# Attention on one core: another order of the score and search pieces within a head

## The reference, cut to what matters

```python
qkv = x @ W_w.T + W_b                                   # x: 2 x 2048 x 256, 16 heads of 16
attn = jnp.einsum('bhqd,bhkd->bhqk', q, k) / jnp.sqrt(jnp.float32(d))
attn = jnp.where(causal[None, None], -jnp.inf, attn)
attn = attn + rpb[rel_idx].transpose(2, 0, 1)[None]     # bias by distance
w = jax.nn.softmax(attn, axis=-1)
o = jnp.einsum('bhqk,bhkd->bhqd', w, v)
```

## Time and profile before

| | |
|---|---|
| median of 3 runs | 2679.14 us (2678.54 to 2680.85) |
| the profiled execution | 2680.85 us, its span 2679.1 us |
| TensorE (PE) busy | 2482.3 us, 93% of the span |
| VectorE (DVE) busy | 1965.3 us, 73% |
| ScalarE (ACT) busy | 1382.1 us, 52% |
| GpSimd (POOL) busy | 1103.8 us, 41% |
| one head of the attention | about 60.5 us |

### The profile page before, as it was taken

How to read it: one execution, slowest core, us unless ns; L and a number is a source line. 1 busy time by engine, 2 the same in 40 slices (tenths; PEclk the granted TensorE clock), 3 DMA queues, 4 the chain that set the end, 5 groups by cost and what they waited for, 6 DMA issues and landing times. The chain is left out here.

```text
span 2679.1 us, 43868 instructions
## 1 busy us (share of the span) xinstructions
PE 2482.3 (93%) x15059; PEld 1557.9 (58%) x15059; DVE 1965.3 (73%) x4039; ACT 1382.1 (52%) x2469; POOL 1103.8 (41%) x1090
## 2 busy tenths in 40 slices
PE   8999999999999999899999996999999999977973
PEld 4433333333333333577777775888888888855762
DVE  3777777777777773456666647999999999973346
ACT  2466666666666666444454536555555555543220
POOL 3522222222222211100001003999999989944543
PEclk9999999999999999999999997999999999987986
DMA  8544323333333411100000000000000000024775
GB/s 244 168 70 75 76 57 57 58 58 58 57 72 70 81 35 66 53 16 17 24 24 16 9 17 8 12 12 12 12 12 12 12 12 12 4 97 146 250 225 170
DMA packets 109601, 166.41 MB, mean 62 GB/s; under 512 B 15876, under 2 KB 74296, under 8 KB 106232
## 3 DMA queue, kind: packets, MB, share of 16 engines
q1 hardware_dynamic: 99064, 143.24, 21.3%
q0 software_dynamic: 6144, 16.79, 2.0%
q10 hardware_dynamic: 4224, 4.19, 0.5%
HBM read 97.66 MB, written 62.01 MB: 60 GB/s over the span
## 5 line engine op out<-in xcount | busy, mean ns | idle before, releaser
L644 ACT ACTIVATE ssm_in_dt<-att_s 128x512 f32<-128x512 f32 (+3 forms) x1280 | 610.0, 535 | 348.1 <-PE att_s L541 183.4
L733 DVE TENSOR_REDUCE att_partmax<-att_s 128x1 f32<-128x512 f32 x768 | 494.1, 685 | 112.7 <-PE att_s L515 66.3
L541 PE MATMUL att_s<-att_qs,att_ks 49*128 49x512 f32 (+3 forms) x1280 | 435.4, 420 | 16.2 <-ACT ssm_in_dt L644 13.8
L515 PE MATMUL att_s<-att_ks,att_qs 49*128 49x512 f32 (+3 forms) x1280 | 435.8, 425 | 4.1 <-DVE att_qs L723 4.1
L1787 POOL TENSOR_TENSOR ssm_cc<-ssm_cc,ssm_h 128x512 f32<-128x512 f32 x256 | 331.8, 1296 | 244.4 <-DVE ssm_h L1844 243.2
L541 PEld LDWEIGHTS att_s<-att_qs,att_ks 49*128 49x128 f32 x1280 | 207.8, 185 | 380.4 <-ACT ssm_in_dt L644 307.5
L432 POOL TENSOR_SCALAR_AFFINE_SELECT ssm_in_dt<-ssm_in_dt 128x256 f32<-128x256 f32 x256 | 104.0, 406 | 619.9 <-ACT ssm_in_dt L644 543.8
L584 PE MATMUL att_o_ps<-ssm_in_dt,att_vst 128*32 128x512 f32 (+3 forms) x2560 | 340.7, 542 | 5.3 <-ACT ssm_in_dt L644 5.3
L1802 POOL TENSOR_TENSOR ssm_out_z<-ssm_out_z,ssm_cc 128x512 f32<-128x512 f32 x256 | 336.8, 1316 | 0.1
L1727 ACT ACTIVATE ssm_cc<-ssm_c_ps,ssm_cur 128x512 f32<-128x512 f32 x256 | 199.3, 778 | 224.7 <-PE ssm_c_ps L1676 224.7
L736 DVE CUSTOM_DVE_ANT_0 att_hid<-att_s,att_hidden 128x512 bf16<-128x512 f32 (+3 forms) x512 | 238.7, 486 | 94.7 <-PE att_s L515 93.9
(11 more groups left out here) (323 smaller groups left out, 4189.6 us busy)
## 6 DMA issues: line engine op xcount, KB each, us to landing
qk_halves<-ssm_in_dt SPq DMA_DIRECT2D x64, 256.0 KB
moe_sorted<-att_hidden SPq DMA_DIRECT2D x31, 512.0 KB, 9.8
moe_rows<-moe_sorted SPq DMA_DIRECT2D x62, 256.0 KB
moe_answers<-moe_mixed SPq DMA_DIRECT2D x62, 256.0 KB
att_far<-bias_tables SPq DMA_DIRECT2D x96, 136.0 KB, 8.2
att_stage_q<-qk_halves SPq DMA_DIRECT2D x96, 128.0 KB, 4.4
att_stage_k<-qk_halves SPq DMA_DIRECT2D x96, 128.0 KB, 6.0
ssm_raw<-in_w_bc SPq DMA_DIRECT2D x30, 256.0 KB, 2.6
```

What stands on the lines that cost most here:

```text
L515: mm = nc.tensor.matmul(s1[:, S1_BANK[at], 0:hi - lo], qs[p % 3][half(b, ROWS), I * P:(I + 1) * P], ks[p % 3][half(b, ROWS), lo:hi], start ...
L541: mm = nc.tensor.matmul(s2[:, turn % RING, 0:hi - lo], ks[p % 3][half(b, ROWS), J * P:(J + 1) * P], qs[p % 3][half(b, ROWS), lo:hi], start ...
L644: nc.scalar.activation(prob[:, b, step % 2, x * CH + lo:(x + 1) * CH], s2[:, turn % RING, 0:CH - lo], ACT.Exp, scale=1.0 / HD).then_inc(s2 ...
L733: nc.vector.tensor_reduce(most, piece, AX, ALU.max).then_inc(s1_read, 1)
```

## The change

It gives other orders to `SCORED` and `SEARCHED`. `SCORED` is now made by a function; the result differs from before in steps 0 and 1 only, where the pieces come in the order of keys. `SEARCHED` keeps its last twelve pieces; of the first 28 most change places. The near groups go with their pieces: they then stand in 0.0, 0.1, 0.3, 1.1, 1.3, 2.1, 3.3, 4.3, 5.0, 5.3, 6.2 and 6.3. The far groups stay where they are. In every slot, the score and the search still have the same number of columns.

```diff
--- before.py
+++ after.py
@@ -125,21 +125,23 @@
 RING = 3
 
 GROUPS_OF_KEYS = ((8, 9), (10, 11), (0,), (1,), (2,), (3,), (4, 12), (5, 13), (6, 14), (7, 15))
-
-
-SCORED = [[(8, 2), (9, 2), (8, 3), (9, 3)], [(11, 2), (10, 2), (10, 3), (11, 3)],
-          [(0, 2), (0, 0), (0, 3), (0, 1)], [(1, 2), (1, 0), (1, 3), (1, 1)],
-          [(2, 2), (2, 0), (2, 3), (2, 1)], [(3, 2), (3, 0), (3, 3), (3, 1)],
-          [(4, 3), (4, 1), (12, 3), (4, 2)], [(5, 3), (5, 1), (13, 3), (5, 2)],
-          [(6, 3), (6, 1), (14, 3), (6, 2)], [(7, 3), (7, 1), (15, 3), (7, 2)]]
-assert [sorted(pieces) for pieces in SCORED] == [[(J, c) for J in keys for c in range(J // TPC, S // CH)] for keys in GROUPS_OF_KEYS]
-SEARCHED = [(15, 0), (14, 3), (15, 1), (15, 2),
-            (12, 3), (13, 3), (13, 0), (12, 2),
-            (8, 0), (15, 3), (14, 0), (14, 2),
-            (12, 1), (10, 2), (12, 0), (13, 2),
-            (9, 0), (9, 2), (11, 1), (11, 2),
-            (13, 1), (8, 2), (10, 0), (9, 1),
-            (11, 0), (8, 1), (14, 1), (10, 1),
+FAR_FIRST = (2, 0, 3, 1)
+
+
+def scored(keys):
+
+    pieces = [(J, c) for J in keys for c in range(J // TPC, S // CH)]
+    return [pieces[n] for n in (FAR_FIRST if keys[0] < FAR else range(len(pieces)))]
+
+
+SCORED = [scored(keys) for keys in GROUPS_OF_KEYS]
+SEARCHED = [(15, 0), (15, 1), (14, 3), (14, 0),
+            (13, 3), (13, 0), (12, 3), (12, 0),
+            (15, 2), (8, 0), (15, 3), (14, 2),
+            (13, 2), (10, 2), (12, 2), (12, 1),
+            (11, 1), (9, 2), (11, 2), (9, 0),
+            (13, 1), (8, 2), (9, 1), (10, 0),
+            (8, 1), (10, 1), (11, 0), (14, 1),
             (7, 0), (6, 1), (2, 0), (7, 1),
             (6, 0), (5, 1), (1, 0), (5, 0),
             (4, 0), (4, 1), (0, 0), (3, 0)]
```

## The result

The changed kernel takes 2802.3 us (median of 4 runs, 2788.1 to 2808.0), against 2678.8 us before (2675.4 to 2680.9): a ratio of 1.0444, 95% interval 1.0421 to 1.0466. The profiled execution took 2793.7 us, its span is 2792.0 us, 112.9 us more than that of before.

What follows compares the result with a forecast made beforehand. TensorE was taken to bound the kernel; 3.65 us at clean places plus net 2.9 us in steps 0 to 2.0, 6.5 us in each of 15 heads, adds 97.5 us: 2776.5 us. Own range 2752 to 2792, wide 2738 to 2800.

Steps and rivals of the forecast that it cites:

- highest sum: Upper bound: five clean places at 0.78 us plus 3.5 us, 7.4 us a head in 15 heads: 111 us, 2790 us.
- signs of being wrong: Among them a head below 64 us, or a granted clock under 1.00 between 190 and 1100 us.
- TensorE sets the pace of a head: Attention heads: a head, 60.5 us, lasts as long as its matmuls; any longer TensorE wait is added whole.
- SCORED at nothing: New score order in steps 0 and 1: same widths paired, moved cuts covered by over 2 us; cost 0.
- Clean places: Near groups at 2.1, 3.3, 4.3, 5.3, 6.3, VectorE empty before: next slot's second search waits; 3.65 us a head.
- Steps 0 to 2.0: Near groups follow closely there: new waits 4.7 us, less 1.8 us of waits before; net 2.9 us a head.
- the walk: TensorE and VectorE traced through steps 0 to 2.0 of a head with profiled durations: new waits together 4.7 us.
- Sum: 3.65 + 2.9 = 6.5 us a head where scores and searches run together, 15 iterations: 97.5 us.
- the clock falls: Waits in steps 0 and 1 drop the clock in every head: 2 us each, +30, about 2807 us; chance 0.07.
- No change: VectorE's slack or a longer queue of work absorbs the heads' waits: about 2679 us; chance 0.03.
- faster: The 1.8 us of waits before in steps 0 and 1 vanish, none come: -27, 2652 us; chance 0.05.
- only the clean places: Steps 0 and 1 absorb their waits, the clean places' remain: +49 to +55, 2730 us; chance 0.07.

Runs made afterwards that it cites:

- s_only: New order of the scores with the old order of the searches, against the kernel before: 2674.8 us, ratio 1.0003.
- late_odd: Kernel before with five swaps in the search order, putting one near group of each of steps 2 to 6 in an odd slot: 2733.7 us, ratio 1.0223.
- late_even: Changed kernel with five swaps in the search order, near groups of steps 2 to 6 back at x.0 and x.2: 2723.8 us, ratio 1.0188.
- half_after: Changed kernel, with VectorE's maximum of pieces with a near group taken over half the columns only: 2723.6 us, ratio 1.0173.
- half_before: Kernel before, with VectorE's maximum of pieces with a near group taken over half the columns only: 2666.1 us, ratio 0.9967.
- half_early: Changed kernel, with maxima of pieces with a near group over half the columns in steps 0 and 1 only: 2744.1 us, ratio 1.0261.
- split_after: Changed kernel, with batch 1's near group in odd slots issued right behind its search, ahead of the sums: 2736.4 us, ratio 1.0235.

## Why the prediction was right

The direction and the mechanism held, and the size came out low. The forecast was 2776.5 us, 97.5 us more than before; 2678.8 x 1.0444 = 2797.8 is 119 us more. That and the profiled 2793.7 lie in the wide range (2738 to 2800), near its end; the median of the four runs, 2802.3, is a little above it. All three are above the forecast's own range (2752 to 2792) and its highest sum, 2790. One of the signs of being wrong came as well: the granted clock in the heads was under 1.00. The steps, one by one:

- **TensorE sets the pace of a head, and a wait is added whole.** Right: nearly the same busy time of VectorE (47.1 us, forecast 47.7), heads longer by the waits.
- **SCORED at nothing.** Right (s_only).
- **Clean places, 5 x 0.73 = 3.65 us.** Right in place and kind, and a little small: 3.9 us, 0.78 each, my upper value. In the rows of the clean place the wait itself is 0.74 us (563.85 + 0.23 to 564.82), as forecast. What I had left out is that the far group follows a search that comes alone after 0.43 us (564.82 to 565.25), and one that came with its partner after 0.31 us. That alone would give 0.86. Against it stands a saving that I had put at nothing: a near group in front of a far group took 0.08 us more than its own 0.45 (405.06 to 405.59 in the earlier trace rows), and at the clean places no far group follows it directly. By this estimate 0.74 + 0.12 - 0.08 = 0.78. The 0.31 us is a row of late_odd, in a slot without a wait:

```profile
466.55 0.39 PE L515 MATMUL att_s<-att_ks,att_qs 49*128 49x512 f32 x1
466.86 0.68 PE L557 MATMUL att_s<-att_far,att_flip_b 64*64 64x384 bf16 x12
```

- **Steps 0 to 2.0, net 2.9 us.** Right: 2.93 to 2.99 us, and the walk is met within 0.11 us at the four points compared above.
- **Sum, 6.5 us a head, 15 heads, 97.5 us.** Heads without a fall: 67.45 - 60.58 = 6.87 us, times 15 = 103 us. The sum was 5% small, mostly for the clean places.
- **The rival "the clock falls", given 0.07.** It came in besides the forecast, in part. I had set it against the forecast as another case, when it was one more term: the waits were enough to bring it, but only in some heads. What it adds: from copy to copy the profiled execution lost 1202.2 - 196.1 = 1006.1 us against 896.8 us (the earlier trace rows show one head; the first and last copy of before start at 191.2 and 1088.0), plus 4.9 us up to the first: 114 us. Eight of the lengths from copy to copy hold the nine falls and are together 13.8 us longer than eight of 67.45 us; the other 100 us are the heads' own, 3 less than 103, since the first and the last of them lose less. A head with a fall takes about 1.6 us more: two heads from 541.0 to 677.5 us take 136.5, of which the first 67.4. My 2 us for a head with a fall was near; nine falls, in eight of the fifteen heads, were what I had not weighed.
- **No change, faster, only the clean places.** All refuted: late_odd and late_even show the price of the clean places and what is left for steps 0 to 2.0, half_after and half_before that VectorE's slack does not absorb it.

The step that missed is thus the pricing of the clock: the sum held nothing for it, and in the profiled execution the falls cost 14 of the 114 us. Before a fall TensorE had been busy 4.20 and 4.43 of 5 us, at 1.00; then the granted clock is near 0.5, the lower level of 1.2 GHz:

```profile
605.00:610.00 5.00, 4.20 (x24) 1.88 (x24) 3.21 (x9) 2.65 (x7) 1.23 (x2) 1.00 0.21 54
610.00:615.00 5.00, 4.43 (x25) 1.86 (x24) 3.36 (x13) 2.15 (x5) 2.84 (x6) 1.00 1.01 138
615.00:618.40 3.40, 3.40 (x15) 0.63 (x14) 0.00 (x0) 0.60 (x1) 0.00 (x0) 0.52 1.13 145
...
580.00:585.00 5.00, 4.52 (x32) 1.95 (x31) 3.11 (x12) 2.99 (x7) 1.71 (x3) 1.00 0.30 70
585.00:590.00 5.00, 4.78 (x34) 1.96 (x30) 1.85 (x8) 1.73 (x5) 2.37 (x5) 1.00 1.05 138
```

The last two rows are steps 0 and 1 of a head of half_early, with no fall behind them. I had argued that waits under 0.9 us with work between would leave the clock alone. They don't: the changed kernel had nine falls, and none once the waits of steps 0 and 1 were shortened (half_early). The five clean waits alone brought none (late_odd). The Trainium skill (TensorE: Matmul & The Clock Gate, section Why this matters for your kernels) asks for matmuls without long idle gaps in mid-kernel. The runs agree that waits bring the falls (half_early), but no single gap here was long: the largest idle time of the whole array in the heads of the changed kernel is under 0.6 us.

The falls also fit the spread of the changed kernel, whose runs lie 0.7% apart: 31 executions ran from 2788.1 us at a mean clock of 0.967 to 2808.0 us at 0.956. late_odd, with heads 3.9 us longer than before and no falls, stays within 2732.6 to 2734.9.

Open: why a fall comes in one head and not in the next with the same waits. The falls begin in steps 0 and 1 of a head, at different places (4.5 to 14.8 us after its start); no experiment here moved that alone. It isn't mere chance: from 615 us on a fall comes in every second head (615.1, 751.6, 888.2 and 1024.7 us), and in late_even in every fourth (387.3, 643.3 and 899.3 us). half_after, with both parts shortened, has none, which fits half_early. split_after doesn't fit so well: its heads are as short as those of half_after, and the clock still fell.

## What to carry to other kernels

Where matmuls of two streams share a small ring of banks, ask for each group that delays a bank's hand-over what stands between it and the first instruction that needs the bank back: the same work costs nothing ahead of 1 us of sums and 0.78 us behind them, at equal counts and equal busy time. Such a list of slots can be walked from a dozen rows (pair 0.23, read 0.69, hand-over 0.05), and such a walk found an order 1% better, too. Price the clock as a term of its own whenever the forecast itself brings many short waits close together.

## What the runs showed of the hardware

- VectorE reads a bank of 512 columns in 0.69 us, but the next read starts 0.61 us after it; ring waits go by the first figure, VectorE's capacity by the second.
- A search and a score of 512 columns side by side in the array take 0.23 us a pair; when the search comes late, as at 564.82 us, the far group starts 0.43 us after it, not 0.31.
- The granted clock fell to 0.5 (1.2 GHz) nine times among heads in which the array was never idle for more than 0.6 us at a stretch; a head with a fall took 1.6 us more.
